# Four transformer layers on one core: the experts' second product as seven block products, score tiles of 32 x 64

## What is computed

```python
def attention(x):                     # 16 heads of 16; layer 0 causal with distance bias, layer 3 not causal
    att = jnp.einsum('bqhd,bkhd->bhqk', q, k) * scale
    w = jax.nn.softmax(att + bias, axis=-1)
    return jnp.einsum('bhqk,bkhd->bqhd', w, v)

def layer_1(u, xt):
    zxbcdt = u @ W_in.T               # z 512, xBC 544, dt 8
    z = zxbcdt[..., :D_INNER]
    xBC = zxbcdt[..., D_INNER:D_INNER + CONV_DIM]
    dt = jax.nn.softplus(zxbcdt[..., -NHEADS:] + dt_bias)
    xBC = silu(depthwise_conv_of_4_taps(xBC) + conv_b)
    y, _ = ssd(x * dt[..., None], A * dt, Bm, Cm, CHUNK)
    y = (y + x * D[:, None]) * silu(z)
    s = rmsnorm(y) @ W_out.T
    gates = entmax_bisect(xt @ Wr + br)                       # 8 experts
    h = jax.nn.relu(jnp.einsum('td,edf->etf', xt, W1) + b1[:, None, :])   # 256 -> 1024
    y = jnp.einsum('etf,efd->etd', h, W2) + b2[:, None, :]                # 1024 -> 256
    return s * silu(jnp.einsum('etd,te->td', y, gates))

x = x + s * g                         # after each of the four layers
```

## Time and profile before

| | |
|---|---|
| time, median of two runs | 4202.14 us (4200.58 and 4203.7) |
| profiled execution | 4203.91 us, its span 4202.1 |
| TensorE busy | 4062.9 us (97%) |
| VectorE, ScalarE, GpSimd busy | 2345.7 (56%), 1888.4 (45%), 646.7 (15%) |
| experts' second product on TensorE | 4096 records of 256 columns, 913.6 us busy |
| loads of w1 (two halves) and w2, per expert | 512 + 512 + 1024 KB |

### The profile page before, as it was taken

One profiled execution on the slowest core, in us unless ns is written; L12 is line 12 of the kernel. 1 busy time (PEld: TensorE's weight loads), 2 busy tenths in 40 slices (PEclk: granted clock), 3 DMA queues, 4 the chain that ended last, 5 costly groups with the idle time before them and its releaser, 6 DMA issues. The chain is left out here.

```text
span 4202.1 us, 57679 instructions
## 1 busy us (share of the span) xinstructions
PE 4062.9 (97%) x21117; PEld 2729.2 (65%) x21117; DVE 2345.7 (56%) x4792; ACT 1888.4 (45%) x3783; POOL 646.7 (15%) x700
## 2 busy tenths in 40 slices
PE   7999999999999999999999999999998998999999
PEld 3444457888888888888888888666665554333333
DVE  6566655334343443434343343577777987667665
ACT  2454455435354444435444353455543221555555
POOL 0122123313133131323213131000000000000000
PEclk8999999999999999999999999999999999999999
DMA  3110102212122221222212121100000001011110
GB/s 90 17 17 16 34 12 99 80 61 98 65 85 79 71 88 61 88 71 87 82 61 88 66 97 47 47 1 1 1 1 22 1 1 26 16 24 21 26 24 22
DMA packets 61888, 198.51 MB, mean 47 GB/s; under 512 B 11257, under 2 KB 21121, under 8 KB 52745
## 3 DMA queue, kind: packets, MB, share of 16 engines
q1 hardware_dynamic: 60784, 194.55, 14.9%
q10 hardware_dynamic: 816, 0.20, 0.0%
HBM read 171.11 MB, written 4.46 MB: 42 GB/s over the span
## 5 line engine op out<-in xcount | busy, mean ns | idle before, releaser
L1211 PE MATMUL l_exp_out<-l_w,l_hidden 128*128 128x256 f32 x4096 | 913.6, 381 | 0.3
L1211 PEld LDWEIGHTS l_exp_out<-l_w,l_hidden 128*128 128x128 f32 x4096 | 769.0, 190 | 116.0 <-issue 9.1
L1369 ACT ACTIVATE l_hidden<-l_hid 128x512 f32<-128x512 f32 x384 | 227.7, 596 | 605.3 <-PE l_hid L1171 604.1
L1747 DVE SCALAR_TENSOR_TENSOR l_moe<-l_exp_out,l_gates,l_moe 128x256 f32<-128x256 f32 x256 | 123.8, 483 | 610.1 <-PE l_exp_out L1211 607.9
L1678 DVE TENSOR_TENSOR l_hidden<-l_hid,l_hidden 128x512 f32<-128x512 f32 x384 | 264.7, 691 | 348.2 <-PE l_hid L1171 343.7
L507 DVE TENSOR_REDUCE l3f_row_max<-l3f_bank 128x1 f32<-128x512 f32 x512 | 327.9, 685 | 176.9 <-PE l3f_bank L387 176.5
L463 ACT ACTIVATE l3f_prob_t<-l3f_bank 128x512 f32<-128x512 f32 x512 | 277.2, 596 | 206.1 <-PE l3f_bank L394 206.0
L1171 PE MATMUL l_hid<-l_x_sums,l_w_sums 128*128 128x256 f32 x1536 | 344.1, 381 | 7.4 <-DVE l_hidden L1678 7.4
L1171 PEld LDWEIGHTS l_hid<-l_x_sums,l_w_sums 128*128 128x128 f32 x1536 | 292.6, 191 | 47.6 <-issue 7.8
L504 DVE CUSTOM_DVE_ANT_0 l_masked<-l_bank,l_mask 128x256 f32<-128x256 f32 (+3 forms) x512 | 226.7, 487 | 161.0 <-PE l_bank L387 160.1
L1381 ACT ACTIVATE l_hidden<-l_hidden,l_w 128x256 f32<-128x256 f32 (+1 forms) x512 | 279.1, 605 | 65.2 <-DVE l_hidden L1678 64.8
(11 more groups left out here) (525 smaller groups left out, 6779.3 us busy)
## 6 DMA issues: line engine op xcount, KB each, us to landing
l_w<-in_w SPq DMA_DIRECT2D x64, 1024.0 KB, 4.8
l_w_first<-in_w SPq DMA_DIRECT2D x64, 512.0 KB
l_w_second<-in_w SPq DMA_DIRECT2D x64, 512.0 KB, 3.7
l_mix<-l_cum SPq DMA_DIRECT2D x32, 512.0 KB, 4.8
l_qk_t<-l_packed SPq DMA_DIRECT2D x128, 64.0 KB
l3f_qk_t<-l3f_packed SPq DMA_DIRECT2D x128, 64.0 KB
all_x<-in_x SPq DMA_DIRECT2D x8, 512.0 KB, 6.0
out_x<-all_x SPq DMA_DIRECT2D x7, 512.0 KB, 3.0
```

The costliest lines, as they stand in the source:

```text
L1211: ins = nc.tensor.matmul(bank[:, 0:C], hidden[:, e % 2, f, j * P:(j + 1) * P], w2[:, e % 2, f, :], start=f == 0, stop=f == HF - 1)
L1369: hid.empty(nc.scalar.activation(hidden_block(e, half_f, x, half_t), pair(bank), ACT.Copy), (e, x, which, turn))
L1747: exp_out.empty(V.scalar_tensor_tensor(moe[:, j, :], bank[:, 0:C], gates[:, j, e:e + 1], moe[:, j, :], ALU.mult, ALU.add), (e, j))
```

## The change

1. **Second product as seven block products** (`out_product`, L1219 of the changed kernel). hidden and w2 are cut in four quarters, and each product has two times four matmuls of 128 columns. Two of four sums of hidden are on GpSimd (`sums_of_hidden`, L1606 and L1607) and two on VectorE (`hidden_sum_2`, `hidden_sum_4`); the four of w2 on GpSimd (`w2_weight_sums`, L1612 to L1617). VectorE adds the products into `moe` in halves of 128 columns: 14 operations per expert instead of 4. To make room in memory, w2, the second half of w1 and `x_dec` have one buffer instead of two.
2. **Convolution within the projections.** xb is computed before z, ScalarE's order follows, and VectorE does the taps in `begin`, between the sums of experts 0 and 1. The routing is cut in parts that stand between the sums of expert 7.
3. **Score tiles of 32 x 64.** Each score matmul of a head is two, for 64 partitions of the result each.

```diff
             bank = flow.open(pe, "score", ("s", w, s))
-            flow.fill(nc.tensor.matmul(bank[:, 0:keys], self.q_t[rows, g, qt * P:(qt + 1) * P], self.k_t[rows, g, 0:keys],
-                                       start=True, stop=True), ("s", w, s))
+            for m in range(0, P, 2 * SLOT):
+                ins = nc.tensor.matmul(bank[m:m + 2 * SLOT, 0:keys], self.q_t[rows, g, qt * P + m:qt * P + m + 2 * SLOT], self.k_t[rows, g, 0:keys],
+                                       start=True, stop=True)
+            flow.fill(ins, ("s", w, s))
 
...
+            for m in range(0, P, 2 * SLOT):
+                ins = nc.tensor.matmul(bank[m:m + 2 * SLOT, 0:T - q.start], self.k_t[rows, g, kb * P + m:kb * P + m + 2 * SLOT], self.q_t[rows, g, q],
+                                       start=True, stop=True)
+            flow.fill(ins, ("t", t, s))
 
...
             def load_second(e):
-                sp.dma_start(w1_second[:, e % 2], w1_dram[e][:, 1]).then_inc(second_loaded[e % 2], 16)
+                sp.dma_start(w1_second[:, :], w1_dram[e][:, 1]).then_inc(second_loaded, 16)
 
             def load_w2(e):
-                sp.dma_start(w2[:, e % 2], w2_dram[e]).then_inc(w2_loaded[e % 2], 16)
+                sp.dma_start(w2[:, :, :], w2_dram[e]).then_inc(w2_loaded, 16)
...
-                if not (is_last and e >= E - 2):
                     hid.wait_filled(sp, b, (e, 1, "a", 3))
-                    load_second((e + 2) % E)
...
-                    if not (is_last and e >= E - 2):
-                        exp_out.wait_filled(sp, b, (e, TJ - 1))
-                        load_w2((e + 2) % E)
+                    if not (is_last and e == E - 1):
+                        exp_out.wait_filled(sp, b, (e, "a", 3))
+                        load_w2((e + 1) % E)
...
+                def out_product(e, which, turn, tokens, weights, start):
+                    bank = exp_out.open(pe, b, (e, which, turn))
+                    for i in range(2):
+                        for k in range(HF // 2):
+                            ins = nc.tensor.matmul(bank[:, i * P:(i + 1) * P], tokens[:, k, i * P:(i + 1) * P], weights[:, k, :],
+                                                   start=start and i == 0 and k == 0, stop=True, skip_group_check=True)
+                    exp_out.fill(ins, (e, which, turn))
+
                 def expert_out(e, between=()):
-                    pe.wait_ge(w2_loaded[e % 2], 16 * (b * (E // 2) + e // 2 + 1))
-                    pe.wait_ge(hidden_ready, RELUS * (b * E + e + 1))
+                    n = b * E + e
+                    pe.wait_ge(w2_loaded, 16 * (n + 1))
+                    pe.wait_ge(hidden_ready, RELUS * (n + 1))
+                    out_product(e, "a", 0, hidden_quarter(e, 0, 0), w2_quarter(0, 0), True)
...
-                    for j in range(TJ):
-                        bank = exp_out.open(pe, b, (e, j))
-                        for f in range(HF):
-                            ins = nc.tensor.matmul(bank[:, 0:C], hidden[:, e % 2, f, j * P:(j + 1) * P], w2[:, e % 2, f, :],
-                                                   start=f == 0, stop=f == HF - 1)
-                        exp_out.fill(ins, (e, j))
-                        if j < len(between):
-                            between[j]()
+                    out_product(e, "b", 0, hidden_quarter(e, 0, 1), w2_quarter(1, 0), True)
+                    if len(between) > 0:
+                        between[0]()
+                    pe.wait_ge(hidden_summed, 4 * n + 3)
+                    pe.wait_ge(w2_summed, 4 * n + 3)
+                    out_product(e, "a", 1, hidden_sums[:, H2], w2_sums[:, R2], False)
+                    out_product(e, "b", 1, hidden_sums[:, H1], w2_sums[:, R1], True)
+                    if len(between) > 1:
+                        between[1]()
+                    out_product(e, "a", 2, hidden_quarter(e, 1, 0), w2_quarter(0, 1), False)
+                    pe.wait_ge(hidden_summed, 4 * n + 4)
+                    out_product(e, "b", 2, hidden_quarter(e, 0, 1), w2_quarter(1, 1), False)
+                    if len(between) > 2:
+                        between[2]()
+                    pe.wait_ge(w2_summed, 4 * n + 4)
+                    out_product(e, "a", 3, hidden_quarter(e, 1, 1), w2_sums[:, R4], False)
...
-                for name, weight in (("z", wz), ("xb", wx)):
+                for name, weight in (("xb", wx), ("z", wz)):
...
+                inner(0)
+                root(b)
+                if b:
+                    exp_out.wait_emptied_through(act, b - 1, [(E - 1, "b", 2), (E - 1, "a", 3)])
+                    nc.scalar.activation(moe[:, :, :], moe[:, :, :], ACT.Silu).then_inc(gate_ready, 1)
+                inner(1)
+                inner(2)
+                inner(3)
+                act.wait_ge(abs_ready, b + 1)
+                nc.scalar.activation(u[:, :, :], u[:, :, :], ACT.Exp).then_inc(act_step, 1)
+                act.wait_ge(act_step, b + 1)
+                nc.scalar.activation(u[:, :, :], u[:, :, :], ACT.Ln, bias=1.0).then_inc(log_ready, 1)
                 for f in range(FT):
                     bank = jobs.wait_filled(act, b, f"z{f}")
                     jobs.empty(nc.scalar.activation(z_act[:, f, :], bank[:, :], ACT.Silu), f"z{f}")
...
+                pool.wait_ge(second_loaded, 16 * (n + 1))
+                V.tensor_tensor(w1_sums[:, S1, :], high, w1_second[:, HALF_F:F], ALU.add).then_inc(w1_summed, 1)
...
+            def sums_of_hidden(n):
+                b, e = divmod(n, E)
+                pool.wait_ge(hidden_ready, RELUS * (n + 1))
                 if n:
...
+                    exp_out.wait_filled(pool, (n - 1) // E, ((n - 1) % E, "b", 1))
+                V.tensor_tensor(hidden_sums[:, H1], hidden_quarter(e, 1, 0), hidden_quarter(e, 1, 1), ALU.add).then_inc(hidden_summed, 1)
+                V.tensor_tensor(hidden_quarter(e, 1, 0), hidden_quarter(e, 0, 0), hidden_quarter(e, 1, 0),
+                                ALU.subtract).then_inc(hidden_summed, 1)
+
+            def w2_weight_sums(n):
+                pool.wait_ge(w2_loaded, 16 * (n + 1))
+                V.tensor_tensor(w2_sums[:, R1], w2_quarter(0, 1), w2_quarter(0, 0), ALU.subtract).then_inc(w2_summed, 1)
+                V.tensor_tensor(w2_quarter(0, 1), w2_quarter(1, 1), w2_quarter(0, 1), ALU.subtract).then_inc(w2_summed, 1)
+                pool.wait_ge(w2_summed, n * 4 + 1)
+                V.tensor_tensor(w2_sums[:, R2], w2_quarter(1, 1), w2_sums[:, R1], ALU.subtract).then_inc(w2_summed, 1)
+                pool.wait_ge(w2_summed, n * 4 + 3)
+                V.tensor_tensor(w2_sums[:, R4], w2_quarter(1, 0), w2_sums[:, R2], ALU.subtract).then_inc(w2_summed, 1)
...
                 scale_c(b, 3)
                 sum_squares(b, 2)
+                w2_weight_sums(n + 5)
                 weight_sums(n + 7)
+                sums_of_hidden(n + 6)
                 sum_squares(b, 3)
+                w2_weight_sums(n + 6)
                 if b < B - 1:
                     weight_sums(n + 8)
                     input_sums(b + 1)
+                sums_of_hidden(n + 7)
+                w2_weight_sums(n + 7)
+                if b < B - 1:
+                    w2_weight_sums(n + 8)
...
+            def hidden_sum_2(it, e):
+                dve.wait_ge(hidden_summed, (it * E + e) * 4 + 2)
+                V.tensor_tensor(hidden_sums[:, H2], hidden_sums[:, H1], hidden_quarter(e, 0, 0), ALU.subtract).then_inc(hidden_summed, 1)
...
+                ring.wait_emptied_through(dve, it, ["xb0", "xb1"])
+                conv_taps(st, 0, 1)
+                ring.wait_emptied_through(dve, it, ["xb2", "xb3"])
+                conv_taps(st, 2)
+                add_11(it, 0)
+                conv_taps(st, 3)
+                add_22(it, 0)
+                add_12(it, 0)
+                conv_taps(st, FT).then_inc(conv_ready, 1)
...
+                def expert_sum(e, which, turn, half_t, half_c):
+                    bank = exp_out.wait_filled(dve, b, (e, which, turn))
+                    c = slice(half_c * P, (half_c + 1) * P)
+                    for i in range(2):
+                        j = 2 * half_t + i
+                        ins = V.scalar_tensor_tensor(moe[:, j, c], bank[:, i * P:(i + 1) * P], gates[:, j, e:e + 1], moe[:, j, c],
+                                                     ALU.mult, ALU.add)
+                    exp_out.empty(ins, (e, which, turn))
...
+                    hidden_sum_2(b, e + 1)
+                    last_sum(e)
```

216 lines of the change are left out of this document (124 added, 92 removed).

## The result

| | before | after |
|---|---|---|
| time, median of two runs | 4202.14 us | 4247.42 us (4242.92 and 4251.92) |
| profiled execution, span | 4203.9, 4202.1 | 4251.9, 4250.2 |
| ratio | | 1.0111, 95% interval 1.0081 to 1.0141 |
| TensorE busy | 4062.9 (97%) | 4009.5 (94%) |

The account below looks back on a forecast made before the run. The prediction took TensorE, 97% busy, to bound the kernel. Its terms, -84.4 - 12.8 + 27.7 + 23.2 + 7.2 + 12.6 + 1.0, summed to -25.5 us: 4178, or 4176 in terms of the median, range 4120 to 4245.

Parts of the forecast that it names:

- block products: Experts' second product in layer 1: 112 records at 111.5 ns, 12.49 for 13.82 us per expert, saving 84 us.
- score tiles: Score matmuls: 25 ns saved in each of 512 groups with two passes, -13 us.
- z and xb on ScalarE: Layer 1 projections: TensorE waits for banks ScalarE empties late, 2.95 us in seven tiles, 7 in the first: +27.7 us.
- w1's second half: Single buffer: expert 1 waits for its load and GpSimd's sums, 2.9 us in each of 8 tiles: +23.2 us.
- squares: After expert 5's second product, chunk 3's sum of squares is late on GpSimd, 0.9 us x 8: +7.2 us.
- output chunks: Tile's end: GpSimd's late hidden sums of expert 7 delay VectorE's output chunks, 1.8 us x 7: +12.6 us.
- last tile, on VectorE: The 7.4 us wait of TensorE in layer 1's last tile grows by 1 us as VectorE gets busier.
- alternatives of 107 and 131: Other prices in ns per 128-column record of the second product: 107 would save 116 us, 131 lose 55 us.
- R1: Rival, chance 0.10: stalls are hidden because GpSimd and ScalarE run ahead; only block products and score tiles count: 4105 us.
- R3: Rival, chance 0.10: matmul and load starts bind in layer 0's short score steps: +78 us, 4254.
- R4: Rival, chance 0.03: the two score halves of a head run in series, each pass streaming twice: about +355 us, 4531.
- R2: Rival, chance 0.12: GpSimd's sums all stretch by a third under contention and three late places double: +43 us, 4219.

Follow-up runs that it names:

- experiment 4: The kernel before with the score tiles of 32 x 64 alone: 4187.4 us, ratio 0.9971.
- e3: The changed kernel with GpSimd's sum of squares of chunk 3 put ahead of expert 6's hidden sums: 4224.8 us.
- e5: The changed kernel without the load of w1's second half for expert 1 of each tile (expert 0's half used again, output differs): 4219.5 us.
- e10_order: e9 with most of VectorE's taps and the norm's statistics moved behind first hidden sums, and GpSimd's w2 sums for expert 7 earlier: 4184.6 us, ratio 0.9973.
- e2: The changed kernel with ScalarE's Exp and Ln put behind the four Silu of the z banks: 4237.6 us.
- e6: The changed kernel with GpSimd's hidden sums of expert 7 ahead of the next tile's weight and input sums: 4239.8 us.
- e9: The changed kernel with z2 and z3 projected between experts 0 and 1, and GpSimd's order changed as in e3 and e6: 4211.1 us.
- e12: e10_order with VectorE's taps of the B and C rows moved from ahead of expert 1's first sum to behind the bias bank copies: 4177.6 us, ratio 0.994.

## Why the prediction was wrong

The sum, term by term. Slow clock and restarts are taken from the profiled spans (4250.2 - 4202.1 = +48).

| term | forecast | measured |
|---|---|---|
| block products | -84 | -84: 12.50 us per expert for 13.81 where nothing stands between, 1.31 x 64 |
| score tiles | -13 | -10 (experiment 4) |
| z and xb on ScalarE | +27.7 | +26.8 (17.9 + 8.9) |
| w1's second half | +23.2 | +19.8 (17.0 + 2.8) |
| squares | +7.2 | +12.6 |
| output chunks | +12.6 | +15.6 |
| last tile, on VectorE | +1.0 | +2.9 (10.3 for 7.4) |
| expert 6, on VectorE | nothing | +12.3 (22.6 - 10.3) |
| expert 0's second product | nothing | +6.3 |
| slow clock behind waits | nothing | +37 |

- **Right:** the beat of 128 columns, which I took at 111.5 ns: 32 records of expert 7 start at 1661.64 and the next at 1665.22, 112 ns. The alternatives of 107 and 131 fall. Right too that the score halves share the array, and the four named places of waits, three of them within 3.4 us of the forecast. R1, R3 and R4 fall (R4 by experiment 4: the second half of a head doesn't wait for the first, so the rule on loads that I had weighed, read as putting the pairs in series, doesn't hold for two column tiles here). Of R2 little is left: GpSimd took 157 us of a tile for my 145, 8% more and not a third.
- **The step that failed** is "the sum": it priced each wait at its length. The missing term is the clock behind the waits, 37 us, by itself half of the 71 us that I was off. The filled waits show it best (22 us less time with no wait shortened, slow clock 14.9 for 43.8). The same wait in a kernel with idle GpSimd and VectorE (slow clock 13.4 for 6.7) and e3 and e5 (31.9 and 37.1 for 43.8) agree with it. I had the clock at 1.00 in the earlier trace rows and took it for a property of the stage; it was one of a stage without waits.
- **Mis-sized:** the waits that VectorE and GpSimd cause, 27.0 us more than forecast in four places (5.4 squares, 3.0 chunks, 12.3 expert 6, 6.3 expert 0's second product); with 4.3 less at w1 and z and 1.9 more in the last tile, 24.6 in all. Part of the cause is seen in the trace, and it is R2's mechanism with another sufferer: VectorE's operations stretch beside GpSimd, up to 3.35 us for 1.22, and I priced all of them by rows from a kernel whose GpSimd was busy for a quarter of the tile. For expert 6 the stretched sum alone is not enough, the order of VectorE's work counts as well: with the sum still at 3.35 us and the statistics moved, 0.5 of 1.7 us stay (`e10_order`). How much of the other three places is due to stretching was not separated. The squares' own sum had a slip besides: 7.35 + 4.7 + 1.2 is 13.25, which is 0.75 us behind 12.5 and not 0.9; the wait measured is 1.6.
- The measured column adds up to +39; the remaining 9 of the 48 us are restarts, by the trace: in the timelines a wait's idle time begins where the last matmul's result is complete, 0.16 us or so behind the beat. Over the 59 listed waits of layer 1 the time from the record ahead to the record behind exceeds that shape's median beat plus the listed wait by 9.8 us, and by 0.5 us over the 2 before. Layer 1 by itself then closes: it is 58.6 us longer, and -84 of matmuls, +96 of waits (104.4 for 8.2), +34 to 37 of slow clock and +9 of restarts make 55 to 58. The rest of the kernel is 10 us shorter, the score tiles.
- "Everything is hidden but these places" failed in one more way: covers. Where a wait was removed, the next stood right behind it (e2, e6, e9, e10, e12). I had treated the places as independent.

## What to carry to other kernels

In a kernel that is bound by TensorE, price a new regular wait of some 2 us at its length and, in a part of the cases (here from one in 7 to 7 in 8), with 1.6 to 1.8 us of slow clock on top; here matmuls nobody needs, put into the wait, won 22 us. Work moved to GpSimd is not free for VectorE: its operations can take over twice their time beside it, so price them by rows that ran beside a busy GpSimd. And a change that saves 1.3 us of matmul 64 times pays only if the order of the other engines is made anew; with it, the same products gave 0.6% instead of losing 1.1%.

## What was not expected of the hardware

- A wait of 2.24 us of TensorE, the same in each tile, was followed by a granted clock of 0.58 over 3.5 us in one tile and 1.00 in the next.
- VectorE's 48x512 tap took 2.00 us beside GpSimd's sums, 0.74 without, while a sum of 128x1024 beside GpSimd's TENSOR_SCALAR (the D term) kept its 1.22 us in 8 of 8 instances; the GpSimd instructions around it took 2.00 and 2.82 us where others of that shape took 1.56, though other VectorE work stood beside them too. An operation with one tensor operand can stretch as well: the first tap took 1.49 us in `e10_order` and 0.53 in the changed kernel.
